# GpSimd's order of work in slots 13 to 63 of a fused cross-attention and spectral feed-forward kernel

## What is computed

```python
def reference(x, ctx_1024, mask, wq, bq, wk, bk, wv, bv, wo, bo, w_freq_real, w_freq_imag, bias):
    # x: (2, 2048, 512), ctx: (2, 128, 512), 16 heads of 32
    h = layernorm(x)
    q, k, v = h @ wq + bq, ctx @ wk + bk, ctx @ wv + bv
    score = einsum('bhqd,bhkd->bhqk', q, k) / sqrt(32) * mask
    score = where(score == 0, -1e9, score)
    x = x + (softmax(score) @ v) @ wo + bo
    y = real(ifft(fft(layernorm(x)) @ (w_freq_real + 1j * w_freq_imag)))
    return x + y + bias
```

## Time and profile before

| | |
|---|---|
| median of 3 runs | 455.94 us (455.06 to 456.8) |
| the profiled execution | 453.91 us, its span 452.1 us |
| PE (TensorE matmul) busy | 433.1 us, 96% of the span |
| DVE (VectorE) busy | 398.3 us, 88% |
| ACT (ScalarE) busy | 368.2 us, 81% |
| POOL (GpSimd) busy | 360.0 us, 80% |
| granted TensorE clock | 0.999 of full |

### The profile page before, as it was taken

The page is one execution under the profiler, slowest core; times in us unless marked ns, Lnnn a source line. Parts: engine busy times, 40 slices in busy tenths (PEclk is TensorE's granted clock), DMA queues, the critical chain, the costliest instruction groups (busy, mean ns, idle before and its releaser), DMA issues.

```text
span 452.1 us, 10893 instructions
## 1 busy us (share of the span) xinstructions
PE 433.1 (96%) x3496; PEld 298.1 (66%) x3496; DVE 398.3 (88%) x532; ACT 368.2 (81%) x1342; POOL 360.0 (80%) x482
## 2 busy tenths in 40 slices
PE   7999898998999999999999999999999999989997
PEld 6796587766666766766666666666666665555444
DVE  2777798798999999999999999999999899999353
ACT  1659878679998989899999898999989899999620
POOL 5788987973879899898989898989898878755763
PEclk9999999999999999999999999999999999999999
DMA  8999744324415455655555544455533424331243
GB/s 270 396 385 214 272 150 113 76 61 112 116 29 141 120 151 109 153 122 145 130 123 113 157 109 137 92 123 153 117 99 73 108 62 117 62 85 24 71 112 122
DMA packets 85286, 60.15 MB, mean 133 GB/s; under 512 B 40141, under 2 KB 72813, under 8 KB 84718
## 3 DMA queue, kind: packets, MB, share of 16 engines
q1 hardware_dynamic: 84508, 59.29, 49.0%
q10 hardware_dynamic: 722, 0.17, 0.2%
HBM read 29.33 MB, written 8.39 MB: 83 GB/s over the span
## 4 chain that ended last, share of the span: by engine, by line
PE 64%; DVE 12%; ACT 7%; issue 6%; POOL 5%; SPq 4%; DMA 2%; DVEq 0%; POOLq 0%; ACTq 0%
PE bank L454 28%; PE bank L459 14%; PE bank L611 8%; PE bank L625 5%; PE scores L599 4%; ACT zs L714 4%; SPq L292 3%; DVE zs L904 3%; DVE zs L897 2%; PE bank L560 2%; DMA xs<-in_x 2%; POOL xtl L1071 1%; ACT pt L723 1%; PE bank L631 1%; DVE x L882 1%
## 5 line engine op out<-in xcount | busy, mean ns | idle before, releaser
L714 ACT ACTIVATE zs<-zs,nbias 128x128 f32<-128x128 f32 x512 | 199.5, 395 | 15.4 <-POOL nbias L1120 14.9
L714 ACT ACTIVATION_READ_ACCUMULATOR zs<-zs,nbias 128x1 f32 x512 | 98.4, 192 | 0.0
L904 DVE SCALAR_TENSOR_TENSOR zs<-zs 128x1024 f32<-128x1024 f32 x64 | 89.6, 1400 | 1.1
L909 DVE TENSOR_REDUCE nmin<-zs 128x8 f32<-128x1024 f32 x64 | 78.1, 1220 | 2.2
L723 ACT COPY pt<-bank 128x512 f32<-128x512 f32 x128 | 67.7, 580 | 13.9 <-PE bank L611 13.7
L897 DVE TENSOR_TENSOR zs<-scores,ms 128x1024 f32<-128x1024 f32 x64 | 78.1, 1220 | 0.1
L611 PE MATMUL bank<-ident,zs 128*128 128x128 f32 x512 | 66.8, 273 | 1.8 <-ACT zs L714 1.8
L1080 POOL TENSOR_TENSOR xs<-xs,bob 128x512 f32<-128x512 f32 (+1 forms) x41 | 42.8, 1047 | 24.9 <-DVE zs L904 21.8
L459 PE MATMUL bank<-xth,wqh 128*128 128x256 f16 x224 | 61.2, 273 | 1.3 <-DVE x L876 1.1
L459 PE MATMUL bank<-xth,wql 128*128 128x256 f16 x224 | 61.1, 273 | 0.0
L459 PE MATMUL bank<-xtl,wqh 128*128 128x256 f16 x224 | 61.1, 273 | 0.0
(11 more groups left out here) (125 smaller groups left out, 911.7 us busy)
## 6 DMA issues: line engine op xcount, KB each, us to landing
xs<-in_x SPq DMA_DIRECT2D x16, 512.0 KB, 4.9
xtr<-in_xt SPq DMA_DIRECT2D x16, 512.0 KB, 4.5
out<-x SPq DMA_DIRECT2D x31, 256.0 KB, 2.4
qs<-qh SPq DMA_DIRECT2D x120, 64.0 KB
lp<-in_lparts SPq DMA_DIRECT2D x4, 1024.0 KB, 9.2
qs<-ql SPq DMA_DIRECT2D x60, 64.0 KB
ms<-in_mask SPq DMA_DIRECT2D x16, 128.0 KB, 2.8
wks<-in_wk SPq DMA_DIRECT2D x2, 512.0 KB, 6.5
```

What stands on the lines that cost most here:

```text
L714: last = act.activation(z, z, ACT.Exp, bias=nbias[:, s % 4, i:i + 1], scale=-NEG, accum_out=zsum[:, s % 4, i:i + 1])
L904: dve.scalar_tensor_tensor(out=z, in0=z, scalar=0.0, in1=z, op0=ALU.is_equal, op1=ALU.subtract).then_inc(eq_done, 1)
L909: dve.tensor_reduce(nmin[:, s % 4, :], zs[:, s % NZ].rearrange("p t h k -> p (t h) k"), AX.X, ALU.min).then_inc(mn_done, 1)
```

## The change

Nothing is added or left out on any engine; only GpSimd's order differs, in slots 13 (`VB`) to 63. Everything before slot 13 and after slot 64 is as it was.

```diff
+VB = 13
...
-                if VS <= v < NS:
+                if VB <= v < NS:
+                    pool.wait_ge(eq_done, v + 1)
+                    if r == 0:
+                        norm_lo2(c - 3, 1)
+                    if r == 2:
+                        norm_lo2(c - 2, 0)
+                    for a in range(5, NC):
+                        if v == 4 * a - 11:
+                            split_lo(a, slice(0, 2), False)
+                    for a in range(3, NC):
+                        if bo_slot(a) == v:
+                            add_bo(a, 0)
+                    bias(v)
+                    if v % 2 == 1:
+                        ctx_lo((v - 5) // 2)
+                    if r == 0:
+                        add_bf(c - 3, 0)
+                        if c + 1 < NC:
+                            scale_mask(c + 1)
+                    if r == 2:
+                        add_bf(c - 3, 1)
+                    for a in range(5, NC):
+                        if v == 4 * a - 10:
+                            split_lo(a, slice(2, 4))
+                    for a in range(3, 12):
+                        if bo_slot(a) == v:
+                            add_bo(a, 1, slice(0, D // 2), False)
+                        if bo_slot(a) + 1 == v:
+                            add_bo(a, 1, slice(D // 2, D))
+                    for a in range(12, NC):
+                        if bo_slot(a) + 1 == v:
+                            add_bo(a, 1)
+                    if v % 2 == 1:
+                        spread((v - 3) // 2)
+                    continue
+                if v == NS:
+                    norm_lo2(c - 3, 1)
+                if VS <= v < VB:
                     pool.wait_ge(eq_done, v + 1)
```

## The result

The changed kernel takes 458.72 us (median of 15 runs, 456.37 to 459.56); the kernel before took 455.94 us (15 runs, 453.68 to 457.73). The ratio is 1.0056, with a 95% interval of 1.0039 to 1.0074: slower, by 2.8 us. The profiled execution took 457.65 us, its span is 455.9.

The account below looks back on a forecast made before the run. PE was taken to bound the middle. +0.8 us there and -1.0 at the end gave 455.94 - 0.2 = 455.7 us, chance 0.55, less than a measurement can tell from no change; 8-in-10 range 453.2 to 459.0.

Parts of the forecast that it names:

- GpSimd's loop drags PE: Rival: the addition ahead of r = 1's bias delays PE, +2.9 us in the middle, nothing back at the end, 458.8 us; chance 0.20.
- The middle is PE's: From 145 to 366 us PE bounds the kernel, at 24.10 us a chunk, since it hardly waits.
- What the edits free: Zero tests of r = 0 and 2 fall to 1.22 us, the reciprocals' copy to 0.60; r = 1's take 1.3 to 1.7.
- the added lateness: Slot 29, bias of r = 1: the moved 128x256 addition makes it 0.4 us later, bounds 0.3 and 0.67.
- The base of the bias: Slot 29's bias stood 13.97 us after the end of slot 27's zero test in the kernel before; the lateness was added to this.
- the base of the loop: Loop from GpSimd's bias through exponentials, queries, masked scores and zero test back: 23.86 us, read while catching up after the lead-in.
- the excess over PE: Middle: the loop with 0.4 us more takes 24.26 against PE's 24.10, dragging PE 0.16 us in each of 8 chunks, 1.3 us.
- the head start: Start of the middle: slot 14's zero test freed (0.38 us) and slot 16's bias 0.1 sooner, 0.5 us gained against the drag.
- The margin: Middle: the drag decides once the added lateness passes 24.10 less 23.86, 0.24 us.
- The end: End stretch: freed zero tests of slots 56, 58 and 62 bring -1.0 us, bounds 0 and -1.6.
- the loss in slot 57: End: a whole b_o addition after `add_bf` and `scale_mask` in slot 56 makes slot 57's bias about 0.5 us later.
- The other edits cost nothing: The moved `norm_lo2`, `add_bf`, b_o halves and second `split_lo` are covered by waits or queues, no time lost.

Follow-up runs that it names:

- Half back: The changed kernel with b_o's second half (128x256) run at the end of r = 2 again, not r = 0; 455.14 us beside 455.99 for the kernel before.
- norm only: The kernel before with only tile 1's `norm_lo2` moved from r = 3 to the next r = 0, ahead of its bias; 455.49 us for 455.40.
- half in r = 1: The changed kernel with b_o's second half one slot later, behind r = 1's bias and low half of the context; 455.06 us for 456.24 before.
- half only: The kernel before with only b_o's second half moved from the end of r = 2 to r = 0, slots from 15 on; 460.17 us for 455.99.
- half dose: The changed kernel with b_o's second half split: 128 columns at the end of r = 0, 128 at the end of r = 2; 454.72 us for 455.40 before.
- The best version: Half back, plus b_o's last three whole additions ahead of the biases of slots 57, 59 and 61; 454.16 us for 455.40 before, again 453.98 for 456.24.

## Why the prediction was wrong, and where it was right

The time fell inside the range (458.7 in 453.2 to 459.0), but not by the forecast. The change is slower by more than its measurement is uncertain, as the rival "GpSimd's loop drags PE" had it at a chance of 0.20, with 458.8 us. Its mechanism is the one the runs show; that its number fits to 0.1 us is in part luck, since it had +2.9 in the middle and nothing at the end, where +3.51 and -0.87 were measured.

- **The middle is PE's: right.** Half back, norm only and half in r = 1 all freed zero tests, and all stood at 24.10 us a chunk. The share of weight loads in half back was 150.88 of 221 us, 68%, with PE busy throughout. The Trainium skill, "Perfetto Trace Analysis", section Identifying the Most-Contended Engine, judges PE's headroom by MFU (the share of peak arithmetic, which the profile does not give) and by this share. By the share PE would have had room; the runs side with the waits.
- **What the edits free: right for r = 0 and for the copy of slot 27.** Slot 28's zero test took 1.25 us, the copy 0.61. **Wrong for r = 1 and 2.** The bias of slot 29 came late enough to push the copy behind it into slot 30's zero test (1.48 us), and slot 29's own was free, 1.22, where I had given it up to 1.7: PE, being late, let VectorE's mask product and zero test come first.
- **The failed step, the added lateness: "0.67 less the 0.1 gained in slot 28 and less 0.2 set up during the zero test: 0.4".** The place and the sign were right, the size was not. Measured against half back, in which the addition alone is elsewhere, the bias is 0.90 us later (14.61 for 13.71). Of it 0.82 is the addition to the next start (220.29 to 221.11). The 0.67 was read where the copy follows; here `ve` follows, and starts only 0.09 after the addition has ended. And nothing was hidden. When the addition is reached, GpSimd has already stood out the zero test, in `scale_mask` (two instructions in 1.87 us; in slot 17 the same two took 0.83). The setup I had counted as saved is saved in both kernels: 0.83 plus 1.22 less 1.87 is 0.18 here, and 0.19 plus 1.22 less the 1.23 of `ve` is 0.18 before. On the loop itself, half only shows 0.72 us (24.58 for 23.86) where 0.4 stood.
- **A second fault, in the same sum.** The base of the bias, 13.97 us, is from a chunk that PE bounds, in which the slack of the loop hides in the waits; the base of the loop, 23.86, is from a chunk that was catching up. In that same chunk of the kernel before, the bias stood at 13.78. Lateness against 13.97 may not be added to a loop that was measured with 13.78.
- **And a third, that ran the other way.** The new order without the addition has a shorter loop than 23.86, since collisions are gone: 23.73 by norm only's catching-up chunk, some 23.6 by difference (half dose). With 0.82 more that is 24.4 to 24.55 us, and the excess over PE 0.3 to 0.45; what I had was 24.26 and 0.16. The drag also lasted nine chunks (slots 15 to 51), not eight, and the head start was 0.36, not 0.5.
- **The order of turns adds the rest.** At first GpSimd came first in r = 1:

```profile
144.83 0.83 POOL L1114 TENSOR_SCALAR ms<-ms,rs 128x128 f32<-128x128 f32 x2
145.73 0.73 POOL L1081 TENSOR_TENSOR xs<-xs,bob 128x256 f32<-128x256 f32 x1
```

  This is GpSimd's timeline of the changed kernel in slot 17, beside the zero test at 145.89 that took 1.65 us; a chunk then took 24.41. In slot 21 VectorE already comes first (its zero test at 169.99 takes 1.22 us, the addition at 170.14 takes 1.66), and from slot 23 on a chunk takes 24.60 to 24.62 in all but one. Why this costs 0.2 more was read from the two timelines, and not tried by itself. Against the kernel before, slots 13 to 15 gave 0.36 us (the head start), slots 15 to 19 cost 0.55, where the kernel before was catching up, slots 19 to 23 cost 0.38, the seven chunks from slot 23 to 51 some 0.5 each, 3.67 in all, and slots 51 to 53 gave 0.73 back: +3.51.
- **The margin was named, and misjudged.** The prediction said the rival decides once the added lateness passes 0.24 us, and set a forecast of 0.4 us on top. With its own bounds of 0.3 to 0.67 the drag was certain and only its size open; it was called no change because the head start (0.5) and the end (1.0) were set against it.
- **The end: right.** -0.87 us for -1.0, with the loss in slot 57 that was foretold (zero tests 57 to 58 are 5.55 us apart for 5.20 before) and the gains around slots 56, 58 and 62. Two details were not foretold: slot 56's zero test is not free (1.41 us), and slot 59's now takes 1.76 (slots 59 to 60 are 4.94 us apart for 4.41; slots 60 to 61, 5.82 for 6.35, make up for it). The best version shows that the loss in slot 57 could be had back.
- **The other edits cost nothing: right,** by half back, which has all edits but one. (Norm only says the same of the middle; its end is 0.36 us longer.)

## What to carry to other kernels

An engine that idles in every round can still carry the loop that sets the round. Before moving an operation into its idle time, find the next instruction behind it that another engine waits for, follow that loop once around, and compare its free length with the bounding engine's (here some 23.6 to 23.7 and 24.1 us): an operation of 0.8 us in front of the awaited instruction cost 3.5 us in all, and behind it nothing. Read the loop's length and the place of its instructions in one and the same stretch, where the loop runs free; in a bound stretch its slack is invisible. And check such a length on a second kernel: an interval between two other points of the round can come out near it by chance. And when a reordering of several edits comes out slightly slower, take out the one that stands in front of the awaited instruction before giving up the rest.

## What was unexpected of the hardware

The two kernels are the same until slot 13, but that slot's zero test stands at 121.22 us before, at 122.27 with the change, and at 124.25 with half back. It goes with the granted clock in part. The stretch from 60 to 80 us, before and then half back, columns as in the earlier trace rows:

```profile
60.00:80.00 20.00, 18.37 (x165) 14.78 (x163) 18.43 (x27) 18.22 (x70) 15.89 (x21) 1.00 0.45 129
```
```profile
60.00:80.00 20.00, 19.16 (x156) 16.07 (x155) 15.89 (x25) 15.12 (x55) 13.92 (x19) 0.93 0.36 102
```

PE was granted 0.93 of its full clock here in one execution and 1.00 in the other, and the same work was done some 3 us later. Of the 13 traces five have such a dip between 50 and 70 us, and in just these five slot 6's zero test stands 1.9 to 3.3 us behind that of before; in the other seven it is at most 1.3 us behind. Which of the two, the dip or the delay, brings about the other is not shown. The 1.05 us of the changed kernel came at a granted clock of 1.00. Executions differ by this before the change has begun; the middle and the end of two kernels should be compared by stretches that start behind it, as the table of the result does.

Where a zero test meets an operation of GpSimd, the times read as if the two took turns by whole instructions, in both directions: a zero test of slots 14 to 50 waits up to 0.45 us for an operation on GpSimd (slot 52's 0.82), and GpSimd's small `ve` of `rstd2`, 0.19 us by itself, took 1.23 us when it met a zero test. The minimum, which reads one operand and writes eight columns, kept to 1219 to 1221 ns whatever ran beside it.
